# Layer 1's normalised features and new state turned by TensorE in fp32 instead of as two f16 parts

## The chip, the cores and the metric

The kernel runs on one core of a Trainium2 chip. The metric is the device time of one execution in microseconds. The profile comes from one further execution. The engines are TensorE (PE; PEld is its loading of weights), VectorE (DVE), ScalarE (ACT), GpSimd (POOL) and SyncE (SP), which issues the DMAs.

## The reference

There are 128 graphs of 128 nodes with 64 features. Layer 0 is an edge network over the adjacency mask. Layer 1 is a message step with a gated (GRU) update. Each has a residual and a layer norm. The part that matters here is layer 1:

```python
m = relu(relu(h @ W1 + b1) @ W2 + b2)
msg = relu(A @ m)
gi, gh = msg @ W_ih.T + b_ih, h @ W_hh.T + b_hh
r, z = sigmoid(i_r + h_r), sigmoid(i_z + h_z)
n = tanh(i_n + r * h_n)
x = layernorm(h + (1 - z) * n + z * h)
```

## The kernel before

Layer 0 works on quarters of four graphs (NQ = 32, index q or t). For each quarter and half, nine rounds a and nine rounds b follow each other: TensorE adds a few products to the running sums in PSUM (`round_a`, `round_b`; profile lines L649 and L903), and VectorE adds the relu of those sums to AC (L1196 for a, L1217 for b). VectorE also makes the next masks DM (`dgen`, L1175), the words WM (L1165) and once per group the table SI (`off`, L1155), which compares with VE, copied by ScalarE (L1513).

Layer 1 works on units of eight graphs (u = 0 to 14, the main units) and at the end on two units of four graphs, for which `late(u)` holds. A unit goes through the steps of `layer1_steps`. The squares of x and the power give the norm factor. `scale1` writes the normalised features X1 (nodes on the partitions, f32). `xg` turns X1 by a product with the identity, so that features stand on the partitions; ScalarE copies the result to XGh (f16) and XG (f32), and GpSimd makes the rest, XGl. `m1`, `m2`, `msg`, the gates, `tanh`, `gd` and `h` follow; `h` leaves the new state GT in f32, features on the partitions. `yt` turns it back and takes off the mean, by a product with the matrix BDC (BDH in f16). ScalarE copies that to Y (L1462), squares it (L1475), GpSimd takes the power (`power2`, L1713 and L1715), and ScalarE scales it to YO (`scale2`, L1484). `store` writes it out.

For main units, `xg` and `yt` work on f16 parts. ScalarE copies X1 to SQ in f16 (`split_x1`, L1632), GpSimd writes X1 - SQ to X1l (L1792), and TensorE adds two products per pair of graphs, with SQ and with X1l. For the new state, ScalarE copies GT to SY (`split_h`, L1626), GpSimd writes GT - SY to GTl (L1797), and TensorE adds the products with SY and GTl. The helper `both` issues each product as two, one for each half of 64 columns of the stationary operand (line L649). SQ and SY serve as targets of the squares too. The late units have no parts: `xg` is a transpose and `yt` one fp32 product.

The order of the work is written out by hand. `main_order` runs over the quarters; the strings ORDER, FIRST, LAST, HEAD and END say which stage takes its next step between which rounds (n, d and e are layer-1 units, r ranks, p preparation, t the tail of a quarter). Every engine follows the same list with its own part, in order, and waits on semaphores. Two PSUM banks, 6 and 7, are handed around by `Banks` for everything besides the rounds; a bank is free again when the copy that empties it is done.

Of the kernel before, what the change touches and what calls it, by code (L numbers as in the profile page):

```python
# [20 lines left out]
F = 64  # L21
H = 192
GB = 8
# [54 lines left out]
).split()  # L78
DENSE = (
# [48 lines left out]
def late(u):  # L128

    return u >= NG - 1  # L130
# [61 lines left out]
def build(nc, adj, adjt, xt, xn, xq, w1, w2, rows, wg, cst, out):  # L192
    ctx = ExitStack()
    with ctx:
# [49 lines left out]
        VE = sb("VE", [128, NB, 2])  # L244
        S2 = sb("S2", [128, NG])
        SQ = sb("SQ", [128, GB, F], F16)
        X1l = sb("X1l", [128, GB, F], F16)
        SY = sb("SY", [128, GB, F], F16)
        GTl = sb("GTl", [128, 512], F16)
        JK = sb("JK", [128, GB * F], BF16)  # L250
        SI = [sb(f"SI{i}", [128, GB, 2, 64], BF16) for i in range(2)]
        OV = [sb(f"OV{i}", [128, GB, 2, 64], BF16) for i in range(2)]
# [36 lines left out]
        XT = XR[1][:].rearrange("p (k a) n -> p k (a n)", a=2)  # L289
        XGf = [t[:].rearrange("p k n -> p (k n)") for t in XG]  # L290
        MSf = MS[:].rearrange("p k n -> p (k n)")
        SYf = SY[:].rearrange("p b n -> p (b n)")
        IHL = wa[:].bitcast(F16).rearrange("p a (k n) -> p a k n", k=3)
        M1f = M1[:].rearrange("p k n -> p (k n)")
        ident = cs[:, CI:CI + 128]
# [34 lines left out]
        def layer1_steps(do, bank, u):  # L330
            def step(name, *args):
                do(name, u, *args)

            step("squares1", 0)
            yield
            step("squares1", 1)
            step("power1")
            yield
            step("scale1", 0)
            yield  # L340
            step("scale1", 1)
            step("split_x1")
            yield
            for k, (name, sem) in enumerate((("xg", "xgc"), ("m1", "m1c"), ("m2", "m2c"), ("msg", "msc"))):
                yield from bank.spare()
                here = bank.take()
                step(name, *here)
                bank.give(here[0], sem, u + 1)
                if k == 0:
                    step("split_xg")  # L350
                if k == 3:
                    step("split_ms")
                if u == NG and k:
                    step(*(("gate_h", 0), ("gate_h", 1), ("gate_hn",))[k - 1], k - 1, [("sy", 9 * NQ)])
                yield
            if u == NG:
                step("gate_i", 0, 0, [])
                step("gt", 2, [])
                step("gate_in", 3, [("sy", 9 * NQ)])
                step("gt_in", 3, [])  # L360
                step("gate_i", 1, 1, [])
            for k in range(2 if u < NG else 0):
                yield from bank.spare()
                here = bank.take()
                step("gate_h", k, *here)
                yield
                step("gate_i", k, *here)
                bank.give(here[0], "sig", 2 * u + k + 1)
                yield
            if u < NG:  # L370
                yield from bank.spare()
                here = bank.take()
                step("gate_hn", *here)
                if not late(u):
                    bank.give(here[0], "hn", u + 1)
                yield
                step("gt", *here)
                if late(u):
                    bank.give(here[0], "gt", 2 * u + 1)
                yield  # L380
                yield from bank.spare()
                here = bank.take()
                step("gate_in", *here)
                if not late(u):
                    bank.give(here[0], "in", u + 1)
                yield
                step("gt_in", *here)
                if late(u):
                    bank.give(here[0], "gt", 2 * u + 2)
                yield  # L390
            step("tanh")
            yield
            step("gd")
            yield
            step("h")
            yield
            if u < NG - 1:
                step("split_h")
                yield
            yield from bank.spare()  # L400
            here = bank.take()
            for k in range(2):
                step("yt", k, *here)
                yield
            if not late(u):
                step("y", *here)
                bank.give(here[0], "y", u + 1)
                yield
            step("squares2", 0, *here)
            yield  # L410
            step("squares2", 1, *here)
            step("power2")
            yield
            step("scale2", 0, *here)
            yield
            step("scale2", 1, *here)
            if late(u):
                bank.give(here[0], "lny", 2 * u + 2)
            yield
            step("store")  # L420
# [233 lines left out]
        def tensor_layer1(e, pe, s):  # L654
# [21 lines left out]
            def xg(u, b, gates):  # L676
                g, c, w, p = unit(u)
                pe.wait_ge(s["dc"], 16)
                pe.wait_ge(s["lnx"], 2 * u + 2)
                for name, v in gates:  # L680
                    pe.wait_ge(s[name], v)
                main_unit = s is main and not late(u)
                if main_unit:
                    pe.wait_ge(s["x1l"], u + 1)
                for k in range(c.start, c.stop, 2):
                    o = PS[:, b, F * k:F * k + 128]
                    if main_unit:
                        both(o, SQ[:, k:k + 2, :].rearrange("p a n -> p (a n)"), idh[:], start=True, stop=False)
                        last = both(o, X1l[:, k:k + 2, :].rearrange("p a n -> p (a n)"), idh[:], start=False, stop=True)
                    else:  # L690
                        last = e.transpose(o, X1[:, k:k + 2, :].rearrange("p a n -> p (a n)"), ident)
                last.then_inc(s["xg"], 1)
# [56 lines left out]

            def yt(u, h, b, gates):  # L750
                g, c, w, p = unit(u)
                main_unit = s is main and not late(u)
                pe.wait_ge(s["h"], u + 1)
                if main_unit:
                    pe.wait_ge(s["hl"], u + 1)
                for name, v in gates:
                    pe.wait_ge(s[name], v)
                half = (c.stop - c.start) // 2
                for k in range(c.start + half * h, c.start + half * h + half, 2):
                    o, n = PS[:, b, F * k:F * k + 128], slice(F * k, F * k + 128)  # L760
                    if main_unit:
                        both(o, SYf[:, n], BDH[:], start=True, stop=False)
                        last = both(o, GTl[:, n], BDH[:], start=False, stop=True)
                    else:
                        last = both(o, GT[:, n], BDC[:], start=True, stop=True)
                last.then_inc(s["yt"], 1)

            return {"xg": xg, "m1": m1, "m2": m2, "msg": msg, "gate_h": gate_h, "gate_i": gate_i,
# [722 lines left out]
        def scalar_main(e):  # L1491
# [126 lines left out]
                ac.wait_ge(s["lnx"], 2 * (g - 1))  # L1618
                e.activation(XR[g % 2][:, c, :].rearrange("p b n -> p (b n)"), PS[:, b, 0:256], ACT.Copy).then_inc(s["xr"], 1)

            def split_h(u):

                ac.wait_ge(s["h"], u + 1)
                ac.wait_ge(s["yt"], 2 * u)
                ac.wait_ge(s["sqy"], 2 * u)
                e.activation(SYf, GT[:], ACT.Copy).then_inc(s["hh"], 1)  # L1626

            def split_x1(u):

                if not late(u):  # L1630
                    ac.wait_ge(s["lnx"], 2 * u + 2)
                    e.activation(SQ[:], X1[:], ACT.Copy).then_inc(s["x1h"], 1)  # L1632

            def fold():
                ac.wait_ge(s["dw"], 16)
                ac.wait_ge(s["s2"], 1)
# [4 lines left out]
            def soon():  # L1641
# [1 line left out]

            follow(main_order, {"soon": soon, "rank_n": rank_n, "split_x": split_x, "off": off, "ov": ov, "rank_t": rank_t, "rank_ov": rank_ov,
                                "x_split": x_split, "x_turn": x_turn, "v": v, "v_low": v_low, "surplus": surplus, "seeds": seeds, "round_a": round_a, "s_ov": s_ov, "out0_c": out0_c,
                                "fold": fold, "split_x1": split_x1, "split_h": split_h,
                                **scalar_layer1(e, ac, s, 2)})

        def scalar_dense(e):
# [100 lines left out]
        def gpsimd_main(e):  # L1750
# [34 lines left out]
                    po.wait_ge(s["gate"], 4 * u)  # L1785
                    e.tensor_tensor(XGl[:], XGf[u % 2], XGh[:], ALU.subtract).then_inc(s["xgl"], 1)

            def split_x1(u):
                if not late(u):
                    po.wait_ge(s["x1h"], u + 1)  # L1790
                    po.wait_ge(s["xg"], u)
                    e.tensor_tensor(X1l[:], X1[:], SQ[:], ALU.subtract).then_inc(s["x1l"], 1)  # L1792

            def split_h(u):
                po.wait_ge(s["hh"], u + 1)
                po.wait_ge(s["yt"], 2 * u)
                e.tensor_tensor(GTl[:], GT[:], SYf, ALU.subtract).then_inc(s["hl"], 1)  # L1797

            def split_ms(u):
                if not late(u):  # L1800
                    po.wait_ge(s["msc"], u + 1)
# [43 lines left out]
            def soon():  # L1845
                hints.append((e, e.mark_branch_hint_location()))

            follow(main_order, {"soon": soon, "setup": setup, "parts": parts, "count": count, "x_split": x_split, "split_x": split_x, "mask": mask, "split_xg": split_xg, "split_ms": split_ms, "split_x1": split_x1, "split_h": split_h, "s_ov": s_ov, "clear": clear, "scale_u": scale_u, "add_u": add_u, "dgen": dgen, **gpsimd_layer1(e, po, s)})

        def gpsimd_dense(e):  # L1850
            follow(dense_order, gpsimd_layer1(e, Lane(e), dense))
# [169 lines left out]
```

## Time and profile before

| what | value |
|---|---|
| median of 3 runs | 804.84 us (804.28 to 804.87) |
| profiled execution | 805.59 us, span 804.1 us |
| mean granted TensorE clock | 0.991 |
| TensorE busy | 695.8 us, 87% |
| VectorE busy | 762.4 us, 95% |
| ScalarE busy | 640.9 us, 80% |
| GpSimd busy | 549.3 us, 68% |

The span goes from the first to the last instruction. Busy times overlap between engines. A matmul's shown duration includes its way through the array, so consecutive matmuls overlap, and the step from one start to the next is what one costs. VectorE's and ScalarE's instructions overlap a little too.

### The profile page before, as it was taken

The page shows a single profiled execution, that of the slowest core. Times are in us where ns is not written, and L with a number is a line of the kernel's source. Part 1 is how long each engine was busy: PE and PEld are TensorE (multiplying, and loading weights), DVE is VectorE, ACT ScalarE, POOL GpSimd, SP SyncE. Part 2 cuts the span into 40 slices and gives each one's busy share as a digit, 9 for nine tenths or more (in the row PEclk, how much of TensorE's full clock was granted, in tenths as well). Part 3 has the DMA queues.
Part 4 walks back from the last instruction along what each step waited for, and adds up shares of the span by engine and source line. Part 5 has one row for each costly group of instructions (what it writes and reads, how often), then busy time and mean ns, then how long its engine had stood idle before and what let it go on. Part 6 is the DMA issues. An engine that isn't in the chain of part 4 may idle for free.

```text
span 804.1 us, 37406 instructions
## 1 busy us (share of the span) xinstructions
PE 695.8 (87%) x15984; PEld 568.7 (71%) x15984; DVE 762.4 (95%) x851; ACT 640.9 (80%) x1897; POOL 549.3 (68%) x625
## 2 busy tenths in 40 slices
PE   3768789889898989989899898989989898988885
PEld 2547677677787867768787777878677687867662
DVE  5799999999999999999999999999999999998983
ACT  5746676888888888888988888888988888887654
POOL 5534445677868677786867779696777969575772
PEclk9999999999999999999999999999999999999998
DMA  5533243233334323323323232433223243222000
GB/s 150 146 105 75 83 100 88 62 75 101 75 100 97 86 76 75 104 73 108 95 81 84 66 113 63 121 81 94 75 65 111 68 120 76 56 61 75 2 15 27
DMA packets 33316, 66.86 MB, mean 83 GB/s; under 512 B 5504, under 2 KB 6272, under 8 KB 33152
## 3 DMA queue, kind: packets, MB, share of 16 engines
q1 hardware_dynamic: 33152, 64.48, 30.3%
q8 instruction: 126, 2.06, 1.1%
q14 instruction: 38, 0.31, 0.1%
HBM read 22.52 MB, written 4.19 MB: 33 GB/s over the span
## 4 chain that ended last, share of the span: by engine, by line
issue 44%; PE 28%; DVE 21%; ACT 3%; DMA 2%; POOL 1%; SPq 0%; DVEq 0%; POOLq 0%
PE PS L649 20%; DVE AC L1196 11%; DVE AC L1217 7%; PE PS L903 3%; PE PS L968 2%; PE PS L723 2%; PE PS L886 1%; DMA VA<-VN 1%; DVE WM L1165 1%; ACT VN L1565 1%; DMA bs<-in_rows 1%; POOL MT L1780 0%; DVE AC L1212 0%; DVE DM L1175 0%; ACT YO L1484 0%
## 5 line engine op out<-in xcount | busy, mean ns | idle before, releaser
L1217 DVE SCALAR_TENSOR_TENSOR AC<-PS,AC 128x1152 f32<-128x1152 f32 (+4 forms) x288 | 333.2, 1157 | 11.6 <-PE PS L649 10.7
L1196 DVE SCALAR_TENSOR_TENSOR AC<-PS,AC 128x1152 f32<-128x1152 f32 (+4 forms) x256 | 291.0, 1137 | 1.6 <-PE PS L903 1.3
L649 PE MATMUL PS<-DM,VA 128*64 128x192 fp8e5 (+1 forms) x2048 | 126.4, 244 | 41.4 <-DVE AC L1196 29.5
L649 PEld LDWEIGHTS PS<-DM,VA 128*64 128x64 f16 x2048 | 81.3, 110 | 77.8 <-DVE AC L1196 49.6
L649 PE MATMUL PS<-DM,VB 128*64 128x192 fp8e5 (+1 forms) x2048 | 123.9, 240 | 0.7 <-DVE AC L1212 0.2
L903 PE MATMUL PS<-DM,VB 128*64 128x192 fp8e5 (+1 forms) x1024 | 85.9, 245 | 23.7 <-DVE AC L1217 19.2
L1175 DVE TENSOR_SCALAR DM<-CW 128x1536 uint16<-128x1536 uint16 (+1 forms) x132 | 96.2, 750 | 1.0 <-DMA CW<-WM 1.0
L649 PEld LDWEIGHTS PS<-DM,VB 128*64 128x64 f16 x2048 | 89.5, 110 | 2.6 <-DVE AC L1217 1.5
L1812 POOL TENSOR_TENSOR XE<-XQ,XT 128x512 f16<-128x512 f32 x32 | 41.3, 1289 | 70.2 <-ACT XT L1552 70.2
L1838 POOL TENSOR_TENSOR AC<-AC,SD 128x512 f32<-128x512 f32 (+1 forms) x62 | 65.3, 1063 | 29.4 <-DVE DM L1175 29.4
L903 PEld LDWEIGHTS PS<-DM,VB 128*64 128x64 f16 x1024 | 45.6, 108 | 54.1 <-DVE AC L1217 26.9
L903 PE MATMUL PS<-DM,VA 128*64 128x192 fp8e5 (+1 forms) x1024 | 83.6, 241 | 0.3
L1831 POOL TENSOR_TENSOR SD<-SD,NNB 128x512 f32<-128x512 f32 x64 | 59.0, 922 | 1.0 <-DVE DM L1175 1.0
L1780 POOL TENSOR_SCALAR MT<-AT 128x1024 bf16<-128x1024 f32 x15 | 41.8, 2784 | 15.1 <-PE PS L649 10.2
L903 PEld LDWEIGHTS PS<-DM,VA 128*64 128x64 f16 x1024 | 49.8, 111 | 1.4 <-DVE AC L1196 0.9
L1565 ACT ACTIVATE VN<-PS 128x384 f16<-128x384 f32 x64 | 31.1, 487 | 23.7 <-PE PS L649 23.6
L1570 ACT ACTIVATE VN<-PS 128x384 f16<-128x384 f32 x64 | 31.2, 488 | 21.8 <-PE PS L649 21.8
L649 PE MATMUL PS<-w2s,AC 128*64 128x64 f32 (+1 forms) x768 | 47.8, 250 | 0.0
L1531 ACT ACTIVATE AM<-PS 64x512 int16<-64x512 f32 x64 | 37.8, 590 | 1.7 <-PE PS L649 1.3
L1542 ACT ACTIVATE AM<-PS 64x256 int16<-64x256 f32 x64 | 24.2, 378 | 18.4 <-PE PS L822 18.0
L1596 ACT ACTIVATE AC<-PS 128x1152 f32<-128x1152 f32 (+1 forms) x32 | 35.4, 1108 | 2.4 <-PE PS L903 2.4
L649 PEld LDWEIGHTS PS<-w2s,AC 128*64 128x64 f32 x768 | 37.3, 138 | 0.0
(240 smaller groups left out, 2067.5 us busy)
## 6 DMA issues: line engine op xcount, KB each, us to landing
CW<-WM SPq DMA_DIRECT2D x128, 160.0 KB, 2.8
XQ<-in_xq SPq DMA_DIRECT2D x32, 256.0 KB, 2.7
VA<-VN SPq DMA_DIRECT2D x64, 128.0 KB, 2.3
VB<-VN SPq DMA_DIRECT2D x64, 128.0 KB, 2.3
AT<-in_adjt SPq DMA_DIRECT2D x15, 512.0 KB, 4.6
XN<-in_xn SPq DMA_DIRECT2D x16, 256.0 KB, 4.4
out<-YO SPq DMA_DIRECT2D x15, 256.0 KB, 2.1
WG<-in_wg SPq DMA_DIRECT2D x1, 515.5 KB, 7.5
```

What stands on the lines that cost most here:

```text
L649: last = e.matmul(o[k], lhs[:, k], rhs, **flags)
L903: last = e.matmul(PS[h:h + 64, b + 2, 256 * (i // 2) + cols.start:256 * (i // 2) + cols.stop], lhs[:, i, k:k + 64], d[:, i, :], start=Fals ...
L1175: e.tensor_scalar(DM[m][:, halves], CW[t % 3][:, halves, first], 6 - 2 * m, 0xC0C0, ALU.logical_shift_left, ALU.bitwise_and).then_inc(s["d ...
L1196: e.scalar_tensor_tensor(t, tiles(PS[:, b + p:b + 3, :])[:, :, cols], 0.0, t, ALU.max, ALU.add).then_inc(s["sx"], 1)
L1217: e.scalar_tensor_tensor(t, tiles(PS[:, r, :])[:, :, cols], 0.0, t, ALU.max, ALU.add).then_inc(s["sy"], 1)
L1531: e.activation(graphs(am[k])[:, :, 64 - 64 * h:192 - 64 * h], src[k], ACT.Copy, scale=2.0, bias=-258.0)
L1565: e.activation(VN[q % 2][:, 0, k:4:2, 0:H], PS[:, b, :].rearrange("p (a n) -> p a n", a=2)[:, :, 0:H], ACT.Copy).then_inc(s["vh"], 1)
L1596: e.activation(ac_[:, 2 * p:6, front], tiles(PS[:, b + p:b + 3, :])[:, :, front], ACT.Relu).then_inc(s["sx"], 1)
L1780: e.tensor_scalar(MT[g % 3][:], AT[g % NA][:], 0.0, None, ALU.is_gt).then_inc(s["mask"], 1)
L1812: e.tensor_tensor(XE[q % 4][:, :, nat], XQ[:], XT0[:], ALU.subtract).then_inc(s["xql"], 1)
L1831: e.tensor_tensor(u, u, NNB[:, 4 * k:4 + 2 * k, :], ALU.mult).then_inc(s["im"], 1)
L1838: e.tensor_tensor(t[:, h, nat], t[:, h, nat], SD[q % 3][:, h, :], ALU.add).then_inc(s["ad"], 1)
```

## The change

`split_x1` and `split_h` go, on ScalarE and on GpSimd, with the buffers X1l and GTl and the four semaphores x1h, x1l, hh and hl. `xg` of a main unit multiplies the f32 X1 with the f32 identity, `yt` the f32 GT with the f32 BDC, once each instead of twice in f16. The `yield` that followed `split_h` stays, so every other step keeps its place in the order. The late units are as before.

```diff
@@ layer1_steps
             step("scale1", 1)
-            step("split_x1")
             yield
...
             if u < NG - 1:
-                step("split_h")
                 yield
@@ tensor_layer1, xg
-                main_unit = s is main and not late(u)
-                if main_unit:
-                    pe.wait_ge(s["x1l"], u + 1)
                 for k in range(c.start, c.stop, 2):
                     o = PS[:, b, F * k:F * k + 128]
-                    if main_unit:
-                        both(o, SQ[:, k:k + 2, :].rearrange("p a n -> p (a n)"), idh[:], start=True, stop=False)
-                        last = both(o, X1l[:, k:k + 2, :].rearrange("p a n -> p (a n)"), idh[:], start=False, stop=True)
+                    if s is main and not late(u):
+                        last = both(o, X1[:, k:k + 2, :].rearrange("p a n -> p (a n)"), ident, start=True, stop=True)
                     else:
                         last = e.transpose(o, X1[:, k:k + 2, :].rearrange("p a n -> p (a n)"), ident)
@@ tensor_layer1, yt
-                if main_unit:
-                    pe.wait_ge(s["hl"], u + 1)
...
-                    if main_unit:
-                        both(o, SYf[:, n], BDH[:], start=True, stop=False)
-                        last = both(o, GTl[:, n], BDH[:], start=False, stop=True)
-                    else:
-                        last = both(o, GT[:, n], BDC[:], start=True, stop=True)
+                    last = both(o, GT[:, n], BDC[:], start=True, stop=True)
@@ scalar_main
-            def split_h(u):
-                ac.wait_ge(s["h"], u + 1)
-                ac.wait_ge(s["yt"], 2 * u)
-                ac.wait_ge(s["sqy"], 2 * u)
-                e.activation(SYf, GT[:], ACT.Copy).then_inc(s["hh"], 1)
-            def split_x1(u):
-                if not late(u):
-                    ac.wait_ge(s["lnx"], 2 * u + 2)
-                    e.activation(SQ[:], X1[:], ACT.Copy).then_inc(s["x1h"], 1)
@@ gpsimd_main
-            def split_x1(u):
-                if not late(u):
-                    po.wait_ge(s["x1h"], u + 1)
-                    po.wait_ge(s["xg"], u)
-                    e.tensor_tensor(X1l[:], X1[:], SQ[:], ALU.subtract).then_inc(s["x1l"], 1)
-            def split_h(u):
-                po.wait_ge(s["hh"], u + 1)
-                po.wait_ge(s["yt"], 2 * u)
-                e.tensor_tensor(GTl[:], GT[:], SYf, ALU.subtract).then_inc(s["hl"], 1)
```

## Rows read from the trace of the kernel before

**Rows 1.** The page's first part: busy time, share of the span, instructions, by engine

```profile
PE 695.8 (87%) x15984; PEld 568.7 (71%) x15984; DVE 762.4 (95%) x851; ACT 640.9 (80%) x1897; POOL 549.3 (68%) x625
```

**Rows 2.** Waits of VectorE, 75 to 770 us: total us, times, longest

```profile
DVE AC L1217 <- PE PS L649: 9.9, 20, 3.3
```

**Rows 3.** One tile's instructions (SQ): count, duration ns min/median/max

```profile
L1632 ACT ACTIVATE SQ<-X x15: 629/630/631, 119.3 to 750.6; 128x512 f16<-128x512 f32 x15
L1792 POOL TENSOR_TENSOR X1l<-X,SQ x15: 1149/1162/1169, 120.1 to 751.3; 128x512 f16<-128x512 f32 x15
```

**Rows 4.** Timeline of TensorE, 216.8 to 218.9 us: start, duration, instruction, [idle]

```profile
216.88 0.22 PE L649 MATMUL PS<-cs,SY 128*64 128x128 f16 x2
217.11 0.33 PE L649 MATMUL PS<-VN,cs 128*64 128x384 f16 x2
217.44 0.22 PE L649 MATMUL PS<-cs,GTl 128*64 128x128 f16 x2
217.63 0.52 PE L649 MATMUL PS<-DM,VA 128*64 128x192 fp8e5 x8
218.15 0.22 PE L649 MATMUL PS<-cs,SQ 128*64 128x128 f16 x2
218.89 0.30 PE L903 MATMUL PS<-DM,VB 128*64 128x128 fp8e5 x4
```

**Rows 5.** Timeline of TensorE, 226.5 to 227.5 us: the m2 step

```profile
226.56 1.04 PE L649 MATMUL PS<-WG,M 128*64 128x128 f32 x16
227.43 0.38 PE L649 MATMUL PS<-SI,cs 128*64 128x512 bf16 x2
```

**Rows 6.** Timeline of VectorE, 218.7 to 225.2 us

```profile
218.76 1.34 DVE L1196 SCALAR_TENSOR_TENSOR AC<-PS,AC 128x1152 f32<-128x1152 f32 x1
220.03 0.94 DVE L1217 SCALAR_TENSOR_TENSOR AC<-PS,AC 128x768 f32<-128x768 f32 x1
...
224.64 0.55 DVE L1175 TENSOR_SCALAR DM<-CW 128x1536 uint16<-128x1536 uint16 x1
225.10 1.22 DVE L1155 TENSOR_TENSOR SI<-cs,VE 128x1024 bf16<-128x1024 bf16 x1
```

**Rows 7.** Timeline of ScalarE, 217.4 to 225 us

```profile
217.48 0.49 ACT L1570 ACTIVATE VN<-PS 128x384 f16<-128x384 f32 x1 [0.67 <-PE PS L649]
217.86 0.59 ACT L1462 ACTIVATE Y<-PS 128x512 f32<-128x512 f32 x1
...
219.46 0.57 ACT L1410 ACTIVATE XGh<-PS 128x512 f16<-128x512 f32 x1
...
223.91 1.06 ACT L1484 ACTIVATE YO<-Y,st 128x64 f32<-128x64 f32 x4
224.88 0.16 ACT L1513 ACTIVATE VE<-PS 128x16 f32<-128x16 f32 x1
```

**Rows 8.** Timeline of GpSimd, 213.9 to 222.3 us

```profile
213.98 1.17 POOL L1792 TENSOR_TENSOR X1l<-X,SQ 128x512 f16<-128x512 f32 x1
...
221.93 0.20 POOL L1713 TENSOR_SCALAR st<-st 128x8 f32<-128x8 f32 x1 [0.18 <-ACT SY L1475]
222.21 1.67 POOL L1715 TENSOR_TENSOR st<-st 128x8 f32<-128x8 f32 x1
```

**Rows 9.** Timeline of GpSimd, 201.5 us, at the start of a dgen step

```profile
201.54 1.52 POOL L1735 TENSOR_TENSOR GT<-XG,GN 128x512 f32<-128x512 f32 x1 [0.69 <-DVE DM L1175]
```

**Rows 10.** Timeline of VectorE, 202.4 us, beside the row above

```profile
202.41 1.06 DVE L1175 TENSOR_SCALAR DM<-CW 128x1536 uint16<-128x1536 uint16 x1
```

**Rows 11.** Timeline of TensorE near the end, 766 to 785 us

```profile
766.22 0.42 PE L649 MATMUL PS<-SHL,OT 128*64 128x64 f16 x16
767.12 0.41 PE L649 MATMUL PS<-XGh,HH 128*64 128x512 f16 x2 [0.25 <-ACT XR L1619]
...
784.44 0.44 PE L1007 MATMUL PS<-on,fb 128*1 128x1 bf16 x12 [0.34 <-ACT XR L1619]
```

**Rows 12.** Timeline of ScalarE near the end, 769.5 us

```profile
769.51 0.66 ACT L1438 ACTIVATE GR<-PS,gbs 128x512 f32<-128x512 f32 x1
```

More of the change, by code:

```diff
@@ L246, in build @@
         SQ = sb("SQ", [128, GB, F], F16)
-        X1l = sb("X1l", [128, GB, F], F16)
         SY = sb("SY", [128, GB, F], F16)
-        GTl = sb("GTl", [128, 512], F16)
         JK = sb("JK", [128, GB * F], BF16)
@@ L291, in build @@
         MSf = MS[:].rearrange("p k n -> p (k n)")
-        SYf = SY[:].rearrange("p b n -> p (b n)")
         IHL = wa[:].bitcast(F16).rearrange("p a (k n) -> p a k n", k=3)
@@ L751, in yt @@
                 g, c, w, p = unit(u)
-                main_unit = s is main and not late(u)
                 pe.wait_ge(s["h"], u + 1)
-                if main_unit:
-                    pe.wait_ge(s["hl"], u + 1)
                 for name, v in gates:
@@ L1645, in scalar_main @@
                                 "x_split": x_split, "x_turn": x_turn, "v": v, "v_low": v_low, "surplus": surplus, "seeds": seeds, "round_a": round_a, "s_ov": s_ov, "out0_c": out0_c,
-                                "fold": fold, "split_x1": split_x1, "split_h": split_h,
+                                "fold": fold,
                                 **scalar_layer1(e, ac, s, 2)})
@@ L1846, in soon @@
                 hints.append((e, e.mark_branch_hint_location()))
-            follow(main_order, {"soon": soon, "setup": setup, "parts": parts, "count": count, "x_split": x_split, "split_x": split_x, "mask": mask, "split_xg": split_xg, "split_ms": split_ms, "split_x1": split_x1, "split_h": split_h, "s_ov": s_ov, "clear": clear, "scale_u": scale_u, "add_u": add_u, "dgen": dgen, **gpsimd_layer1(e, po, s)})
+            follow(main_order, {"soon": soon, "setup": setup, "parts": parts, "count": count, "x_split": x_split, "split_x": split_x, "mask": mask, "split_xg": split_xg, "split_ms": split_ms, "s_ov": s_ov, "clear": clear, "scale_u": scale_u, "add_u": add_u, "dgen": dgen, **gpsimd_layer1(e, po, s)})
         def gpsimd_dense(e):
```

2 rows, old and new, of the table MAIN are left out of this document.

## The prediction

> **What bounds the kernel now.** First the page's first part [rows 1]: VectorE is busy 95% of the span, TensorE 87%, ScalarE 80%, GpSimd 68%. Then VectorE's waits in the steady stretch, 75 to 770 us: TensorE holds it up for 9.9 us in 20 waits, 3.3 us of it in one [rows 2], and nothing else appreciably. So nearly all of those 695 us is VectorE's own work, and there is hardly any waiting to be won back. An edit on another engine shows in the time only where it makes VectorE wait, or shortens a VectorE instruction. The third view is the timeline of each engine over one unit of layer 1. The pattern repeats every 46.6 us, so one period can be read closely and multiplied. The last 25 us are different: there the chain runs through TensorE, ScalarE and GpSimd in turn.
>
> **What is removed.** Per main unit (15 of them) ScalarE loses two copies to f16 and GpSimd two subtractions. The x1 pair takes 0.63 and 1.16 us [rows 3]; the h pair has the same shapes. That is 15 × 2 × 0.63 = 19 us of ScalarE and 15 × 2 × 1.16 = 35 us of GpSimd. I cost all of it at nothing. The x1 subtraction runs at 213.98 to 215.15 and the h one right behind it, so both parts are ready by about 216.3, but TensorE begins the h product only at 216.88 and the x1 product at 218.15 [rows 4, 8], because the written order puts them there. Neither waits for its low part. What is queued behind on GpSimd comes about 2.3 us earlier, and then waits for ScalarE anyway: power2's first instruction has idle time before it, ended by ScalarE's squares [rows 8]. No DMA is moved, and no wait is added.
>
> **What the fp32 products cost TensorE.** A half of yt in f16, eight matmuls, goes from 216.88 to 217.11, 0.23 us; a whole unit's turn (yt, and xg likewise) is twice that, 0.46. The fp32 form stands in the trace as well: m2 does the same eight calls (64 columns of f32 weights, 128 f32 columns moving), recorded as sixteen, from 226.56 to the next instruction at 227.43 [rows 5], 0.87 us. So xg and yt each go from 0.46 to 0.87, a half of yt from 0.23 to 0.44. That is +0.41 × 2 × 15 = +12.3 us of TensorE work. The ends round this price: 0.87 is the step to the next instruction, 1.04 the span with the last matmul's tail; the low end is no rise at all (0.46), if what limits such short matmuls were their issue. I take 0.87, as the shape is identical.
>
> **Does VectorE wait for those 12 us?** I follow one period [rows 4, 6]. yt ended its issue at 217.49 (its last pair starts at 217.44), and the round at 217.63 waited for VectorE, so 0.14 us was free. With +0.42 the round starts at 217.91, 0.28 late. It takes 0.52 to issue and about 0.16 more for its last result: 218.59. VectorE wants it at 218.76: 0.17 to spare. xg then runs 218.43 to 219.30, and the next round, at 218.89 before, starts 0.41 late and delivers at about 219.83; VectorE wants it at 220.03. Still 0.2 to spare, and the rounds behind it have gaps of their own. So the matmul rounds stay in time, by 0.1 to 0.2 us. If that cover were gone, every 0.1 us would cost 1.3 us in all.
>
> **The longer way round, through ScalarE.** The half of yt before the v_low matmul (VN, 217.11) pushes that by 0.21 and with it the copy of VN on ScalarE, 217.48 to 217.69; the next instruction there could start 0.38 later, 218.07. v_low costs 0.16 (the second half went from 217.27 to 217.50), so the second half now starts at 217.48, and a half delivers its last result 1.04 - 0.44 = 0.60 after its start: 218.08, and 0.04 for the semaphore (217.11 + 0.33 = 217.44 to 217.48 is such a step). So the Y copy moves from 217.86 to 218.12, +0.26 [rows 4, 7]. Queued behind it in ScalarE's order are four squares, the two copies of XG (219.46 on), the copy of the next VN, four more squares. Between them the timeline shows no idle time, so the last square is 0.26 late, and so is power2 on GpSimd, which waited for exactly that (221.93; its second instruction ends at 223.88) [rows 8]. scale2 starts at 223.91, right behind power2's end, and behind four of its instructions stands the copy of VE, 224.88 to 225.04 [rows 7]. VectorE's SI instruction starts at 225.10 and reads VE [rows 6]. With 0.04 for the semaphore only 0.02 us is free there. The delay of 0.26 arrives at VectorE as 0.24. Between m1's relu and scale2 ScalarE has slack, but power2 is on the path beside it, so the slack does not help. After SI the engines are late together and keep their places to each other, so I see nothing that gives it back. SI follows a yt in this way 12 times (178.5 to 691.0 us): 12 × 0.24 = 2.9 us. The ends of this term: 0 if a gap that the timeline rounds away absorbs it, and 12 × 0.42 = 5.0 us if the whole growth of yt passes.
>
> **The end.** In the last two yt turns the order is half of yt, then the SHL product that completes out0, then the other half. The XR copy waits for SHL, and TensorE waits for XR (0.25 us idle before 767.12, 0.34 before 784.44) [rows 11]. Each time the first half's +0.21 goes straight to the path. The first time the Y copy is 0.38 late, as both halves stand before it, and so the sigmoid at 769.51 to 770.17 [rows 12], for whose bank TensorE waits at about 770.2; there some 0.16 more is lost. The sum: 0.21 + 0.16 + 0.21 = 0.6 us. The removed h copy and subtraction are not on this path, as TensorE waits for XR, not for them.
>
> **Sum.** 2.9 + 0.6 = +3.5 us. The profiled execution took 805.59 us (span 804.1), 0.75 above the median of the runs shown, so its like would be 809.1; on the median 804.84 it gives 808.3 us.
>
> **Rivals.** *The order absorbs it.* If the SI link isn't tight, only the end is left: 804.84 + 0.6 = 805.4. For it: the engine gaps are read to 0.01 us, and the link rests on a 0.02 us margin. Against it: no idle time is shown anywhere between Y and the squares. Chance 0.18.
>
> *The rounds overflow.* If an fp32 turn costs 1.04 instead of 0.87, since its tail isn't hidden when weights and moving data change sides (X1 and GT stationary), the round at 218.89 becomes 0.75 late and VectorE waits 0.15 to 0.2 us in 14 units, 2.5 us, and Y is 0.17 later 12 times, 2.0 us: 808.3 + 4.5 = 812.8. For it: the margins of 0.17 and 0.2. Against it: m2 has the same sides. Chance 0.13.
>
> *The other side: faster, through VectorE's short instructions.* A dgen instruction of VectorE takes 0.55 us alone (224.64) [rows 6] and 1.06 beside GpSimd's gd step (202.41) [rows 9, 10]. Taking 35 us off GpSimd could pull its remaining steps out from under these: 13 periods × 0.51 us = 6.6 us won, 3.1 net, 801.7 us. It decides as soon as one GpSimd step that now overlaps a dgen instruction is let go earlier by the missing subtractions. Against it: that step starts after 0.69 us of idle time ended by VectorE's dgen itself, so it isn't held by a backlog, and where the two subtractions stood (213.98 to 216.3) VectorE ran its PSUM steps. Chance 0.06. The page "SBUF — State Buffer" of the Trainium skill (Who interferes with whom) says that a VectorE instruction with at most one input in SBUF and outside the two-port modes doesn't contend with GpSimd. The step at 218.76, with GpSimd in small work, takes 1.34, and I find the same 1.34 over the subtractions; by that rule, as by the rows, removing them there gives VectorE nothing. 
>
> **How the numbers follow.** Forecast 808.3 us, chance 0.63, its own range 806.6 to 810.5 (its terms from 1.2 + 0.6 to 5.0 + 0.6). The rest: absorbed 0.18 (805.4), overflow 0.13 (812.8), faster 0.06 (801.7). The range of 8 in 10 leaves out the faster case and the upper part of the overflow and reaches to the absorbed one: 805.0 to 812.0. What a measurement of this kernel tells from no change is about 0.2%, 1.6 us. Faster than 803.2: the third rival and a little for the unseen, 0.07. Within: the absorbed case and a small part of the forecast, 0.21. Slower than 806.4: 0.72.
>
> **What would show it.** Eight xg calls in about 0.87 us of TensorE; Y about 0.26 later against VectorE's rounds; an idle time of about 0.24 us on VectorE before SI, ended by ScalarE's VE copy, 12 times; no new waits in the rounds at 218.8 and 220.0; dgen instructions as long as before; the period 46.8 instead of 46.6 us; XR 0.2 later in the last two turns. It is wrong if SI has no wait before it (absorbed), if the rounds do (overflow), or if fewer dgen instructions are long (faster).

## The result, and the profile after

Five runs of the changed kernel took 807.73 to 809.09 us, median 808.52; the kernel before in the same comparison 804.84. The ratio is 1.0044, 95% interval 1.0029 to 1.0058: slower by 3.7 us. The forecast was 808.3 in a range of 805.0 to 812.0. The profiled execution took 807.73 us, span 806.3, the lowest of the five.

The first part of the page after:

```profile
PE 701.6 (87%) x15984; PEld 580.0 (72%) x15984; DVE 764.1 (95%) x851; ACT 624.5 (77%) x1867; POOL 515.2 (64%) x595
```

Against [rows 1], ScalarE lost 16 us and GpSimd 34 us of busy time, where 19 and 35 were counted (ScalarE's records overlap a little, so its busy time falls by less than their sum). TensorE shows 5.8 us more, not 12.3: busy time of overlapping matmuls is no measure of what they hold up, the steps between starts are. VectorE's waits from 75 to 770 us (total, times, longest), to be held against [rows 2]:

```profile
DVE AC L1201 <- PE PS L644: 9.2, 18, 3.3
DVE SI L1139 <- ACT VE L1497: 2.0, 12, 0.2
```

The second line is new: 12 waits before SI, for the VE copy. The timeline of TensorE over the same slots as [rows 4]; the whole run is 1.23 us earlier here, so 216.88 of before answers to 215.65:

```profile
215.66 0.60 PE L644 MATMUL PS<-cs,GT 128*64 128x128 f32 x8
216.09 0.33 PE L644 MATMUL PS<-VN,cs 128*64 128x384 f16 x2
216.25 0.60 PE L644 MATMUL PS<-cs,GT 128*64 128x128 f32 x8
216.69 0.50 PE L644 MATMUL PS<-DM,VA 128*64 128x192 fp8e5 x8
217.19 1.04 PE L644 MATMUL PS<-cs,X 128*64 128x128 f32 x16
218.06 0.28 PE L887 MATMUL PS<-DM,VB 128*64 128x128 fp8e5 x4
```

Half a yt takes 0.43 us (215.66 to 216.09), xg 0.87 (217.19 to 218.06). The rounds at 216.69 and 218.06 are 0.29 and 0.40 late, and VectorE doesn't notice. Its timeline, as [rows 6]:

```profile
217.53 1.35 DVE L1180 SCALAR_TENSOR_TENSOR AC<-PS,AC 128x1152 f32<-128x1152 f32 x1
218.79 0.95 DVE L1201 SCALAR_TENSOR_TENSOR AC<-PS,AC 128x768 f32<-128x768 f32 x1
...
223.41 0.55 DVE L1159 TENSOR_SCALAR DM<-CW 128x1536 uint16<-128x1536 uint16 x1
224.13 1.23 DVE L1139 TENSOR_TENSOR SI<-cs,VE 128x1024 bf16<-128x1024 bf16 x1 [0.17 <-ACT VE L1497]
```

The rounds at 217.53 and 218.79 are where they were, 1.23 and 1.24 before 218.76 and 220.03. SI starts at 224.13, 0.72 after the dgen instruction instead of 0.46: 0.26 late. ScalarE, as [rows 7]:

```profile
216.46 0.49 ACT L1554 ACTIVATE VN<-PS 128x384 f16<-128x384 f32 x1 [0.88 <-PE PS L644]
216.91 0.60 ACT L1446 ACTIVATE Y<-PS 128x512 f32<-128x512 f32 x1
...
218.51 0.57 ACT L1394 ACTIVATE XGh<-PS 128x512 f16<-128x512 f32 x1
...
222.97 1.07 ACT L1468 ACTIVATE YO<-Y,st 128x64 f32<-128x64 f32 x4 [0.41 <-POOL st L1686]
223.94 0.16 ACT L1497 ACTIVATE VE<-PS 128x16 f32<-128x16 f32 x1
```

With 1.23 added, VN's copy is 0.21 late, Y 0.28, the XG copy 0.28, scale2 and VE 0.29. GpSimd's power2, as [rows 8]:

```profile
220.98 0.20 POOL L1684 TENSOR_SCALAR st<-st 128x8 f32<-128x8 f32 x1 [0.18 <-ACT SY L1459]
221.26 1.67 POOL L1686 TENSOR_TENSOR st<-st 128x8 f32<-128x8 f32 x1
```

It is 0.28 late and passes the delay on: scale2 now waits for it, 0.41 us.

Where the 2.2 us between the two spans lie is best read from one fixed point to the next, in the profiled execution of each kernel (us). The columns: the start of the SI after the first yt (of unit 0); from there to the last SI, eleven periods; from the last SI to the start of the second of the last XR copies; and to the end of VectorE's last instruction.

| kernel | SI after the first yt at | to last SI | last SI to last XR | last SI to end |
|---|---|---|---|---|
| before | 178.51 | 512.51 | 92.89 | 110.71 |
| after | 177.27 | 515.35 | 93.69 | 111.24 |
| xg_only | 177.70 | 512.60 | 92.89 | 110.28 |
| yt_only | 178.18 | 515.42 | 93.73 | 111.29 |
| yt_twice | 177.63 | 515.44 | 93.72 | 111.71 |
| ve_first | 178.73 | 514.30 | 93.88 | 111.46 |
| scale_later | 177.40 | 512.66 | 93.79 | 111.34 |
| yt_late | 178.39 | 512.48 | 93.51 | 111.06 |
| scale_quiet | 179.13 | 510.13 | 93.39 | 110.94 |
| quiet_before | 179.57 | 517.30 | 92.50 | 110.38 |
| scale_tail | 177.26 | 512.55 | 101.24 | 124.21 |
| quiet | 177.78 | 508.40 | 99.47 | 122.97 |

The eleven periods cost +2.84 us, 0.258 each; with the first SI that makes 3.1. The end costs +0.80 up to XR; the last column shows only +0.53, because the granted clock gives something back there (see "The end" below). The first column scatters by 2.3 us with no pattern that I can name, and it alone makes the profiled execution of after look 1.2 us better. The steady stretch is steadier: before, xg_only, yt_late and scale_later agree within 0.2 us there.

### The profile page after: what moved, and what is told of

It is laid out like the page before. It is cut to its first block, busy times and chain, and to the rows that moved or that the text cites. A ratio compares the mean times of both kernels' runs of the same rounds, so it can differ in the third digit from the quotient of the medians.

```text
span 806.3 us, 37333 instructions
## 1 busy us (share of the span) xinstructions
PE 701.6 (87%) x15984; PEld 580.0 (72%) x15984; DVE 764.1 (95%) x851; ACT 624.5 (77%) x1867; POOL 515.2 (64%) x595
## 4 chain that ended last, share of the span: by engine, by line
issue 36%; DVE 25%; PE 23%; ACT 10%; POOL 4%; DMA 1%; SPq 0%; DVEq 0%; POOLq 0%
PE PS L644 16%; DVE AC L1201 10%; DVE AC L1180 9%; ACT SY L1459 3%; PE PS L887 3%; POOL st L1686 3%; DVE SI L1139 2%; PE PS L952 2%; PE PS L714 2%; ACT YO L1468 1%; ACT VN L1549 1%; ACT Y L1446 1%; PE PS L870 1%; DVE WM L1149 1%; DMA bs<-in_rows 1%
## 5 line engine op out<-in xcount | busy, mean ns | idle before, releaser
L644 PEld LDWEIGHTS PS<-DM,VA 128*64 128x64 f16 x2048 | 82.4, 109 | 71.2 <-DVE AC L1180 46.3
L1757 POOL TENSOR_TENSOR XGl<-XG,XGh 128x512 f16<-128x512 f32 x15 | 17.4, 1160 | 49.6 <-ACT XG L1395 49.6
L1603 ACT ACTIVATE XR<-PS 128x256 f32<-128x256 f32 x32 | 12.3, 384 | 41.4 <-PE PS L644 41.3
```

The lines of the kernel that those rows point to most:

```text
L644: last = e.matmul(o[k], lhs[:, k], rhs, **flags)
```

## The experiments

The ratios are to the kernel before, with their 95% intervals.

**xg_only.** X1 in fp32, the new state as before.

```diff
-            step("split_x1")
-                if main_unit:
-                    pe.wait_ge(s["x1l"], u + 1)
...
-                        both(o, SQ[:, k:k + 2, :]..., idh[:], start=True, stop=False)
-                        last = both(o, X1l[:, k:k + 2, :]..., idh[:], start=False, stop=True)
+                        last = both(o, X1[:, k:k + 2, :]..., ident, start=True, stop=True)
```

> Only the normalised features are turned in fp32; the new state keeps its f16 parts, its split and its two products. Theory (the late VE copy): the fp32 turn of X1 adds 0.41 us to TensorE, which the matmul rounds absorb, and it moves no instruction of ScalarE that leads to VE. VectorE has no wait before SI; the time is that of before, 804.8 us, within 0.5. Rival (rounds overflow, or TensorE work counts as such): half of the change's 3.7 us, so 806.7 us, with new waits of VectorE for TensorE in the rounds after xg.

Measured: 804.82 us against 805.32, ratio 0.9993 (0.9984 to 1.0002). No SI wait is listed. The xg half of the change is free: 0.41 us more of TensorE, 15 times, cost nothing. Nor do a gain and a cost cancel here: in the period behind the first SI of the table, VectorE's rounds from 33 us on, beside the removed subtraction and xg, stand within 0.01 us of where they stood in before.

**yt_only.** GT in fp32, X1 as before.

```diff
-                step("split_h")
-                if main_unit:
-                    pe.wait_ge(s["hl"], u + 1)
...
-                    if main_unit:
-                        both(o, SYf[:, n], BDH[:], start=True, stop=False)
-                        last = both(o, GTl[:, n], BDH[:], start=False, stop=True)
-                    else:
-                        last = both(o, GT[:, n], BDC[:], start=True, stop=True)
+                    last = both(o, GT[:, n], BDC[:], start=True, stop=True)
```

> Only the new state is turned in fp32; X1 keeps its f16 parts. Theory (the late VE copy): all of the change's cost is here, 808.5 us; SI waits 0.16 us for the VE copy 12 times and begins 0.26 us later against the round before; the last two turns cost their 0.6. Rival (half of the cost each): 806.7 us.

Measured: 809.77 us, ratio 1.0052 (1.0038 to 1.0065). VectorE's waits:

```profile
DVE SI L1148 <- ACT VE L1506: 2.1, 12, 0.2
```

All of the cost is here, and the table's columns repeat those of after.

**yt_twice.** The kernel before; the four f16 products of yt issued twice.

```diff
+                        for again in range(2):
-                        both(o, SYf[:, n], BDH[:], start=True, stop=False)
-                        last = both(o, GTl[:, n], BDH[:], start=False, stop=True)
+                            both(o, SYf[:, n], BDH[:], start=True, stop=False)
+                            last = both(o, GTl[:, n], BDH[:], start=False, stop=True)
```

> The kernel before, with the four f16 products of yt issued twice (the second set writes the same sums again): 0.46 us more of TensorE in each yt, as f16, with all splits and buffers in place. Theory: what counts is when yt ends, not the number format nor the removed copies, so this costs what the change costs, or a little more, 808.8 us, with SI waiting for VE 12 times. Rival (something of fp32 itself, or of the removed steps and buffers, makes the cost): 804.8 us, or a pattern of waits other than at SI.

Measured: 809.32 us, ratio 1.0046 (1.0032 to 1.0059).

```profile
DVE SI L1156 <- ACT VE L1514: 2.1, 12, 0.2
```

The same waits and the same 515.4 us over the eleven periods, with no fp32 and nothing removed. So it is the time at which yt ends. And as yt_only, without the split of the new state, takes what yt_twice takes with it, that removed split is worth nothing either.

**ve_first.** The changed kernel; off ahead of scale2's first half.

```diff
-    (..., "pc", "d", "", "e0r1"),
+    (..., "pc", "d", "", "0re1"),
```

> The changed kernel with one letter of the order moved: the off step (TensorE's product, ScalarE's copy of VE, VectorE's SI) stands ahead of the first half of scale2 instead of behind it. Theory: the VE copy no longer waits for power2, SI has no wait, and 12 x 0.26 = 3.1 us go; what is left is the end: 805.4 us. Rival (VectorE then waits for the next late thing, NNB or SD behind scale2, which is now later by the VE copy only): 807 to 808.5 us.

Measured: 808.34 us, ratio 1.0031 (1.0020 to 1.0043). The SI wait is gone, but over the eleven periods only 1.05 of 2.84 us are won. TensorE's waits show a line that after doesn't have, and its timeline where it is:

```profile
PE PS L644 <- ACT MS L1415: 2.8, 12, 0.2
```

```profile
278.56 0.41 PE L644 MATMUL PS<-MT,cs 128*64 128x512 bf16 x2 [0.23 <-ACT MS L1415]
278.80 0.33 PE L887 MATMUL PS<-DM,VB 128*64 128x192 fp8e5 x4
```

The rank product MT waits for a bank which the MS copy empties, and the MS copy stands 6.6 us further down ScalarE's queue than the VE copy (271.25 and 277.90). VectorE's rounds behind it start 0.16 us later against SI than in before. That is the rival's case in kind and size, though it named NNB or SD and not MS: a packed queue carries the delay on. My theory of one tight link was too narrow.

**scale_later.** The changed kernel; scale2's first half behind the next XR copy.

```diff
-    (..., "pc", "d", "", "e0r1"),
-    (..., "t", "et", "pr", "dlendpn", ...),
+    (..., "pc", "d", "", "0r1"),
+    (..., "t", "ete", "pr", "dlendpn", ...),
...
-    ("deesbbt2bd", ...),
+    ("deeesbbt2bd", ...),
```

> Moving only the off step ahead (ve_first) took the wait before SI away but gave 1.0 us, not 3.1: ScalarE's queue behind power2 is packed, so the copies behind scale2 came late too, and TensorE waited 0.2 us for the copy of MS. Here the first half of scale2 leaves that place altogether and goes behind the next XR copy, where ScalarE idles 0.97 us. Theory (a packed ScalarE queue from Y to MS carries the delay of yt): the queue is then early, both waits are gone, the period is 46.6 us again and the time 805.4 us, the end's 0.6 over before. Rival (each fix only uncovers the next late thing): a period of 46.7 to 46.8 and 807 to 808.5 us.

Measured: 805.93 us against 805.16, ratio 1.0011 (1.0002 to 1.0020). The eleven periods take 512.66 us, the kernel before's 512.51. So 2.7 of the steady stretch's 2.84 us were the packed queue, and the end is left. One thing was unforeseen. Without scale2 in front, ScalarE's XT copy and so GpSimd's x_split come earlier against VectorE's dgen pair; that pair takes 1.35 us instead of 1.97, but the time won is lost at once, in a wait for TensorE:

```profile
276.71 1.36 DVE L1180 SCALAR_TENSOR_TENSOR AC<-PS,AC 128x1152 f32<-128x1152 f32 x1 [0.63 <-PE PS L887]
```

**scale_tail.** scale_later; in the last two yt turns SHL's product ahead of both halves.

```diff
-    (..., "ttendbdted", ...),
+    (..., "ttndbdteed", ...),
-END = ("tltltdn", "n", "n", "t", "ddl", ...
+END = ("tltltn", "n", "n", "t", "dddl", ...
```

> scale_later, and in the last two yt turns the SHL product of out0 stands ahead of both halves of yt instead of between them. Theory: the half in front of SHL cost 0.21 in each turn over its 0.23 of before, and the XR copy is on the path both times; so the end gets shorter by 2 x 0.44 us and by part of the 0.16 of the late sigmoid: 804.5 us. Rival (the end's path runs through Y and the squares instead, which this leaves as late as before or makes 0.1 later): 805.4 us or a little more.

Measured: 818.43 us, ratio 1.0170 (1.0156 to 1.0184). It was forecast at 804.5 and tells nothing of the question. In the kernel's order a step that finds no free bank of the two skips its letter. So most likely holding the banks in another order shifted the whole end (12 to 13 us longer in the table); VectorE now waits 3.1 us in one of the last rounds and 5.7 us for the gates.

```profile
DVE GT L1076 <- PE PS L644: 5.7, 1, 5.7
```

**quiet, quiet_before, scale_quiet.** GpSimd waits for the last dgen of the quarter at two places, on scale_tail, on the kernel before and on scale_later.

```diff
                 po.wait_ge(s["o0"], q - 3)
+                po.wait_ge(s["dd"], RD * q if q > 1 else 0)
...
                     po.wait_ge(s["sy"], 9 * q + 9)
+                    if q % 2 == 0 and k == 0 and q < NQ - 2:
+                        po.wait_ge(s["dd"], RD * (q + 2) + 4)
```

> scale_tail, and GpSimd in addition waits for the last dgen instruction of the quarter before its x_split step, and in even quarters before the first add of the surplus. My third rival said that GpSimd's steps beside dgen are worth something: one dgen of 1.19 us and one of about 1.4 instead of 0.55 in each period of two quarters, both with VectorE work right behind. Theory: 0.64 + 0.86 = 1.5 us per period, 13 periods, 19 us: 785 us, if the 35 us that the change freed on GpSimd take up the later start. Rival (GpSimd becomes late for h, SHL or the XGl part and TensorE and VectorE wait for it): 800 us or over, with waits of TensorE for GpSimd.

> The kernel before, with the same two added waits of GpSimd. It tells whether the gain of quiet needs what the change freed. If GpSimd's 68% are no hindrance: 19 us less than before, 786 us. If the splits of x1 and h, which stand behind the delayed steps in GpSimd's queue, come too late for xg and yt: TensorE waits at them, and the time is 3 us or more above that of quiet.

> scale_later with GpSimd's two added waits, and the end's order as it was. In the run quiet the waits gave 0.4 us a period instead of 1.5, because TensorE is as late as the long dgen instructions there: VectorE waited for TensorE instead. But 0.4 us remained, between the second SI and the last it was 3.9 us less than scale_later. Theory: the same here, without the end that was spoiled by the other order: 805.9 - 4 to 5 us, so 801.5 us, below both kernels. Rival (the gain of quiet in the steady stretch came with a loss at its end): 804 us or over.

Measured: quiet 817.82 us, ratio 1.0173 (1.0147 to 1.0198), with the end spoiled as in scale_tail. quiet_before 811.08 us, 1.0078 (1.0064 to 1.0092). scale_quiet 803.94 us against 805.28, 0.9989 (0.9974 to 1.0003). All three forecasts (785, 786 and 801.5 us) were missed; 804 or over, the rival for scale_quiet, is nearer. The dgen instructions did get short: 1.19 to 0.55 us, the pair 1.36 to 1.02. But VectorE then waits for TensorE at both places: 0.64 and 0.34 us won, the period only 0.42 shorter (46.60 to 46.18 from scale_tail to quiet), not 1.5. Of the 0.86 us expected from the pair, 0.61 had come about in scale_later already, and been lost there. In scale_quiet most periods are 46.2 us as well, but four in the middle of the run take 46.3 to 47.2; why is open, and its twelve times scatter more than the others (800.9 to 806.1). VectorE's waits over the whole of scale_quiet, then of quiet_before:

```profile
DVE AC L1180 <- PE PS L887: 13.6, 15, 0.9
```

```profile
DVE SI L1155 <- ACT VE L1513: 4.6, 11, 0.4
```

The second shows what the splits do where GpSimd has no time for them. In quiet_before the split of the new state ends late, and yt begins only 0.10 us behind it; TensorE has 12 such idle times, 6.4 us in all:

```profile
452.58 1.16 POOL L1797 TENSOR_TENSOR GTl<-GT,SY 128x512 f16<-128x512 f32 x1
453.84 0.25 PE L649 MATMUL PS<-cs,SY 128*64 128x128 f16 x2 [0.54 <-issue]
```

That comes through to VE and SI 11 times, and the kernel is 6 us slower than before. scale_quiet is 1.3 us faster than before by the medians, which is not clear of noise. It differs from quiet_before in the place of scale2 and in the number format too, so the 7 us between them are not the splits' alone.

**yt_late.** The kernel before; fp32 in yt for u = 13 and 14 alone.

```diff
             if u < NG - 1:
-                step("split_h")
+                if u < NG - 3:
+                    step("split_h")
                 yield
...
-                main_unit = s is main and not late(u)
+                main_unit = s is main and u < NG - 3
```

> The kernel before, with the new state turned in fp32 only for the last two main units (u = 13 and 14), whose yt turns stand in the end stretch; units 0 to 12 keep their f16 parts. Theory: no wait at SI, the end costs its 0.6 us, so 0.6 over before. By the trace of the whole change I now expect the last XR copy 0.64 us later against the last SI, not 0.84, as 0.2 of that arises earlier. Rival (the end recovers everything, or the steady part costs nothing and the end all): the time of before, or 3 us more.

Measured: 805.97 us against 805.28, ratio 1.0005 (0.9996 to 1.0014): by itself not clear of noise. The profile shows no SI wait from 75 to 770 us, 512.48 us in the steady stretch, and the last XR 0.62 us later against the last SI, as expected.

## Why the prediction was right, point by point

**Removed work at nothing**: right. xg_only takes away 15 x (0.63 + 1.16) = 27 us of ScalarE and GpSimd work and gains nothing measurable; yt_only against yt_twice shows the same of the other half. The rule of the page "SBUF — State Buffer" of the Trainium skill (Who interferes with whom), that a VectorE instruction with one input in SBUF outside the two-port modes doesn't contend with GpSimd, agrees with the trace: VectorE's rounds beside the two subtractions (214.97 and 216.23) took 1.34 us before, and the same two take 1.34 now, with only small GpSimd work beside them.

**Price of the fp32 product**: right. 0.87 was taken for eight calls, 0.87 measured; 0.43 for a half, 0.44 taken.

**Rounds stay in time**: right. Both rounds hold their place against VectorE; xg_only shows it without the rest.

**The way through Y, power2, scale2 and VE**: right in mechanism and size. Taken: Y 0.26 and SI 0.24 late, 12 times, 2.9 us. Measured: Y 0.28, SI 0.26, 12 waits, 3.1 us. VectorE loses all but 0.02 us of what ScalarE does. Too narrow was the reason that nothing would give it back: not only VE, but ScalarE's whole queue down to MS is tight. It changes nothing in the sum, but ve_first had to fail by it.

One place does give time back, which I had overlooked. In before, one round came 0.28 us late against SI (TensorE had waited for a DMA), and the WM instruction behind it, which otherwise takes 1.26 us beside GpSimd's steps at this place, took 0.97. The next round stood where it always stands:

```profile
303.46 0.97 DVE L1165 TENSOR_TENSOR WM<-c,AM 128x1280 uint16<-128x1280 uint16 x1
```

In one period of after a round is 0.46 late, WM takes 0.82, and that delay is gone too. So a delay of VectorE alone is absorbed there. The delay at SI is not: GpSimd is late with it, and WM keeps its 1.26 us.

**A 13th place was overlooked.** After the yt of unit 12 no SI follows, and I counted nothing. ScalarE is 0.29 late there as well, so GpSimd's SHL step comes 0.29 later against the last SI, stands beside a dgen instruction for longer, and that takes 1.20 us instead of 0.93:

```profile
741.90 0.67 POOL L1821 TENSOR_TENSOR SHL<-SO,SHL 128x256 f16<-128x256 f32 x1 [1.47 <-ACT SHL L1612]
743.19 0.93 DVE L1175 TENSOR_SCALAR DM<-CW 128x1536 uint16<-128x1536 uint16 x1
```

```profile
743.79 0.68 POOL L1781 TENSOR_TENSOR SHL<-SO,SHL 128x256 f16<-128x256 f32 x1 [1.74 <-ACT SHL L1596]
744.80 1.20 DVE L1159 TENSOR_SCALAR DM<-CW 128x1536 uint16<-128x1536 uint16 x1
```

The first two lines are before, the others after. The round behind it starts 0.17 us later against the last SI. The runs bear it out: this dgen instruction takes 1.20 or 1.21 us in yt_only, yt_twice and ve_first, where the yt of unit 12 ends late, and 0.92 in xg_only and yt_late, where it doesn't. In scale_later it takes 1.30 and the round is 0.28 late; there scale2's halves still stand in front at this place.

**The end.** 0.58 taken, 0.80 measured up to the last XR. Of these, 0.17 is the 13th place. yt_late has the rest, 0.62: 0.21 at the first XR, 0.20 more where TensorE waits for the sigmoid's bank (770.2 in before), 0.21 at the second XR, where 0.21, 0.16 and 0.21 were taken. TensorE there, as [rows 11]:

```profile
767.78 0.60 PE L644 MATMUL PS<-cs,GT 128*64 128x128 f32 x8
768.22 0.42 PE L644 MATMUL PS<-SHL,OT 128*64 128x64 f16 x16
768.47 0.63 PE L644 MATMUL PS<-cs,GT 128*64 128x128 f32 x8
769.11 0.41 PE L644 MATMUL PS<-XGh,HH 128*64 128x512 f16 x2
```

Behind the last XR the sum missed another 0.20: both halves of the last yt stand before the Y copy, and TensorE's next product now waits for that copy.

```profile
787.43 0.65 PE L644 MATMUL PS<-XG,WG 128*64 128x256 f32 x4 [0.16 <-ACT Y L1446]
```

From there on after is 1.00 us later against the last SI than before. It keeps these 1.00 us until the last unit's yt, an fp32 product in both kernels (eight records), which took 1.12 us in before and 0.66 in after:

```profile
797.83 1.12 PE L649 MATMUL PS<-cs,GT 128*64 128x128 f32 x8 [2.98 <-DVE GT L1116]
798.00:799.00 1.00, 0.95 (x8) 0.55 (x8) 0.00 (x0) 0.00 (x1) 0.64 (x1) 0.50 0.00 0
```

```profile
800.42 0.66 PE L644 MATMUL PS<-cs,GT 128*64 128x128 f32 x8 [2.98 <-DVE GT L1100]
800.00:801.00 1.00, 0.58 (x8) 0.42 (x8) 0.37 (x1) 0.00 (x0) 0.95 (x1) 1.00 0.00 0
```

The second line of each is a stretch with the busy time of TensorE, its weight loads, VectorE, ScalarE and GpSimd, the granted clock, the DMA share and GB/s. In before the clock had fallen to the level of 1.2 GHz (0.50) at about 797.0, while TensorE was idle ahead of this yt. In after it still stood at 2.4 GHz (1.00) and fell at about 801.8, behind it. That gives back 0.46 of the 1.00 us, and VectorE's last instruction is 0.53 later. Two other executions show the same. before and xg_only stand at the same places up to this yt; xg_only's takes 0.70, and all behind it is 0.43 earlier. yt_twice's takes 1.12 at 0.50, as in before, and its end is 1.00 us longer than before's. What decides whether the clock falls ahead of this yt or behind it, no run shows.

**The sum.** At an equal clock the parts measured are 3.1 for the way to SI and 1.0 for the end, 4.1 us, where 2.9 and 0.6 were taken. The runs gave 3.7 (after), 4.5 (yt_only) and 4.0 (yt_twice) by the medians, and the intervals of all three hold 4.1. So that 808.3 came within 0.2 us of 808.52 is in part luck: two places of the end were left out, 0.17 and 0.20, and the clock gave 0.46 back in the profiled execution. The steady part was no luck. The lower end of the forecast's own range has no working: it takes 1.2 us for the SI term, where the paragraph on that term says 0.

**The rivals.** Absorbed: refuted by 12 waits. Overflow: refuted, the price was 0.87. Faster through dgen: the condition didn't come about; in the steady stretch the long instructions stayed long. The price I gave it, 0.51 us per period for the dgen at 202.41, was wrong in any case: the round behind that dgen waits for TensorE, before as after, so a shorter dgen there would only have made this wait longer:

```profile
202.57 1.36 DVE L1201 SCALAR_TENSOR_TENSOR AC<-PS,AC 128x1152 f32<-128x1152 f32 x1 [0.32 <-PE PS L644]
```

The run quiet showed the same at two other places.

## What to carry to other kernels

A step's cost off the bottleneck engine is found by following what is queued behind its result, on every engine, until someone has idle time; here 0.26 us travelled through the squares and copies of ScalarE's queue and a power on GpSimd to an instruction of VectorE. Where a queue is packed, moving one late copy forward uncovers the next; what helped here was to take work out of the queue ahead of both and put it where the engine idles. A long instruction is worth shortening only if what follows it is ready: look what the engine behind would be late with first.

## What the runs showed of the hardware

A short uint16 instruction of VectorE (dgen) takes 0.55 us alone, 1.06 to 1.19 beside a GpSimd step, and 0.93 or 1.20 by how far the two overlap. GpSimd suffers as well: the first instruction of its gd step takes 1.52 beside dgen [rows 9] and 1.27 at the least in the run. VectorE's WM instruction (uint16, both inputs in SBUF) takes 0.82 alone and 1.26 beside GpSimd's steps. The last unit's yt in fp32 (eight records, 64 weight columns, 128 moving) takes 0.66 us at a granted clock of 1.00 and 1.12 at 0.50. Over the last 8 us of the run the mean granted clock was 0.56 in before, 0.66 in xg_only and 0.74 in after, for nearly the same work.
